# Graph layer with a maximum on one NeuronCore: gathered rows normalized on ScalarE instead of GpSimd, record ranks compared without a subtraction, a normalization's shifts in one operation

## What is computed

```python
h = max(layernorm(x), 0)
# layer 0: for every edge (row -> col)
feat = concat(h[col], h[row] - h[col])
messages = relu(feat @ W1 + b1) @ W2 + b2
x = x + segment_max(messages, col)          # 0 where a node has no edge
h = max(layernorm(x), 0)
# layer 1: averages of projected neighbours both ways, then a GRU cell
a_in  = segment_mean((h @ W_in.T + b_in)[src], dst)
a_out = segment_mean((h @ W_out.T + b_out)[dst], src)
x = x + gru_cell(concat(a_in, a_out), h)
```

## Time and profile before

| | us |
|---|---|
| median of three runs | 4011.75 |
| lowest and highest | 4011.28, 4018.98 |
| the profiled execution | 4021.37 |
| its span (first to last instruction) | 4019.6 |
| PE busy | 3058.4 (76%) |
| DVE busy | 3394.0 (84%) |
| ACT busy | 2061.9 (51%) |
| POOL busy | 2698.1 (67%) |

### The profile page before, as it was taken

The page is one execution under the profiler, slowest core; times in us unless marked ns, Lnnn a source line. Parts: engine busy times, 40 slices in busy tenths (PEclk is TensorE's granted clock), DMA queues, the critical chain, the costliest instruction groups (busy, mean ns, idle before and its releaser), DMA issues. The chain is left out here.

```text
span 4019.6 us, 91086 instructions
## 1 busy us (share of the span) xinstructions
PE 3058.4 (76%) x18561; PEld 1953.7 (49%) x18561; DVE 3394.0 (84%) x14919; ACT 2061.9 (51%) x4963; POOL 2698.1 (67%) x2895
## 2 busy tenths in 40 slices
PE   0244427777777777777777399999999999999998
PEld 0011116566555555555666255555555555555554
DVE  8844439999999999999999488888888888888888
ACT  0000017777677677767777144545544554555454
POOL 0266647777777777777777376666666666666664
...
GB/s 48 1 1 1 1 31 120 119 117 119 111 120 119 113 121 120 118 112 119 119 117 120 85 170 169 173 168 168 174 169 168 169 174 168 168 171 171 169 168 133
DMA packets 513673, 492.31 MB, mean 122 GB/s; under 512 B 218528, under 2 KB 487328, under 8 KB 513152
## 3 DMA queue, kind: packets, MB, share of 16 engines
...
## 5 line engine op out<-in xcount | busy, mean ns | idle before, releaser
L2536 POOL DMA_INDIRECT s_rows<-h_dram,s_idx x1044 | 989.3, 948 | 534.6 <-DVE s_idx L2743 277.3
L2111 POOL DMA_INDIRECT m_xg<-in_x_dram,m_idx x522 | 519.1, 994 | 143.8 <-issue 72.0
L2646 PE MATMUL sp_g<-s_wb,s_hT 128*128 128x512 f16 x2349 | 608.5, 379 | 0.0
L2659 PE MATMUL sp_g<-s_proj,s_onehot 128*128 128x384 f16 x3132 | 594.2, 326 | 0.0
L2636 PE MATMUL sp_p<-s_lhs,s_dT 128*128 128x384 f32 x1044 | 463.8, 526 | 93.6 <-DVE s_proj L2771 93.0
L2567 ACT ACTIVATE s_proj<-sp_p,s_share 128x384 f16<-128x384 f32 (+1 forms) x522 | 298.0, 571 | 377.6 <-PE sp_p L2636 377.6
L2120 POOL TENSOR_SCALAR m_h<-m_xg,m_mv,m_rs 128x128 f32<-128x128 f32 x522 | 477.9, 919 | 17.1 <-DVE m_rs L2319 6.4
L2127 POOL TENSOR_TENSOR m_q_rows<-m_x1s,m_h1s 128x384 f32<-128x384 f32 x261 | 259.7, 995 | 247.3 <-ACT m_h1s L2184 137.1
L710 POOL DMA_INDIRECT lists_src<-p_ent,p_pos x256 | 249.4, 974 | 254.8 <-issue 223.1
L2659 PEld LDWEIGHTS sp_g<-s_proj,s_onehot 128*128 128x128 f16 x3132 | 306.3, 98 | 231.2 <-issue 58.4
L2771 DVE SCALAR_TENSOR_TENSOR s_proj<-sp_p,s_share,s_proj 128x384 f16<-128x384 f32 (+1 forms) x522 | 320.1, 613 | 75.2 <-ACT s_proj L2567 75.2
...
...
## 6 DMA issues: line engine op xcount, KB each, us to landing
m_x<-in_x_dram SPq DMA_DIRECT2D x261, 192.0 KB
h_dram<-m_h1s SPq DMA_DIRECT2D x261, 192.0 KB
q_dram<-m_q_rows SPq DMA_DIRECT2D x261, 192.0 KB
s_h_rows<-h_dram SPq DMA_DIRECT2D x261, 192.0 KB
s_q_rows<-q_dram SPq DMA_DIRECT2D x261, 192.0 KB
out_dram<-s_out_rows SPq DMA_DIRECT2D x261, 192.0 KB
s_erow<-lists_dst SPq DMA_DIRECT2D x261, 128.0 KB
s_erow<-lists_src SPq DMA_DIRECT2D x261, 128.0 KB
```

The costliest lines, as they stand in the source:

```text
L2111: G_.indirect_dma_start(out=xg[:, st.slot(4), q, :], out_offset=None, in_=x[:, :], in_offset=bass.IndirectOffsetOnAxis(ap=idx[:, st.slot(4 ...
L2536: G_.indirect_dma_start(out=rows[:, s4, q, :], out_offset=None, in_=h1_dram[0:G * GROUP, :], in_offset=bass.IndirectOffsetOnAxis(ap=idx[:, ...
L2646: T.matmul(bank[:, t, :], hT[:, st.slot(4), of, t * P:(t + 1) * P], wb[:, w, :], start=(q == 0), stop=False, skip_group_check=True)
L2659: mm = T.matmul(ps_g[s2][:, t, 0:H3], onehot[:, st.slot(4), k, t * P:(t + 1) * P], proj[:, s2, k, w, :], start=False, stop=(k == 1 and w = ...
```

## The change

In `layer_max_sorted`, in four places:

- GpSimd's `normalize` is gone. ACT's `normalize` runs over five blocks instead of three; the last two come from `xg`. The semaphore `hg` is gone, and everybody who waited for it waits for five counts of `h` instead of three.
- `shifts` is one operation, minus one times `mv` times `rs`, over all five columns, in place of three operations on one column each. Both `mv` and `rs` are now inputs that are tensors; before, `rs` was a scalar read per partition.
- `shifts1` likewise, over three columns.
- `edge_ranks`, the tile `slot` and its semaphore are gone. `edge_slots` adds `first_rank` to `iota_slot` and compares with the record's own rank, with two scalars read per partition.

On DVE's list `(2, edge_ranks)` falls out and nothing else moves.

```diff
@@ gpsimd @@
                 def gather(st):
                     after(pool, "idx", st, per=2)
-                    after(pool, "h", st, per=3, back=4)
-                    after(pool, "hg", st, per=2, back=4)
+                    after(pool, "h", st, per=5, back=4)
...
-                def normalize(st):
-                    pool.wait_ge(S["rs"], st.count(4) - 3)
-                    after(pool, "tn", st, back=2)
-                    pool.sem_inc(S["go"], 1)
-                    for q in range(2):
-                        G_.tensor_scalar(h[:, st.slot(2), 3 + q, :], xg[:, st.slot(4), q, :], mv[:, st.slot(2), 3 + q, 0:1], rs[:, st.slot(4), 3 + q:4 + q],
-                                         ALU.subtract, ALU.mult).then_inc(S["hg"], 1)
...
-                fixed_loop(pool, G, [(6, gather), (8, normalize), (13, carried)], SPAN)
+                fixed_loop(pool, G, [(6, gather), (13, carried)], SPAN)
@@ scalar @@
                 def normalize(st):
-                    after(act, "rs", st, per=4)
+                    after(act, "rs", st, per=2)
                     after(act, "tn", st, back=2)
-                    for q in range(TILES):
-                        A.activation(h[:, st.slot(2), q, :], x3[:, st.slot(UN), q, :], ACT.Identity, bias=nm[:, st.slot(4), q:q + 1],
+                    for q in range(5):
+                        rows = x3[:, st.slot(UN), q, :] if q < TILES else xg[:, st.slot(4), q - TILES, :]
+                        A.activation(h[:, st.slot(2), q, :], rows, ACT.Identity, bias=nm[:, st.slot(4), q:q + 1],
                                      scale=rs[:, st.slot(4), q:q + 1]).then_inc(S["h"], 1)
@@ vector @@
-                def edge_ranks(st):
-                    landed(v, d_win, st)
-                    after(v, "sorted", st, back=UN)
-                    V.tensor_scalar(slot[:, st.slot(UN), :], win[:, st.slot(UN), :, 0], first_rank[:, bass.ds(st.t, 1)], None,
-                                    ALU.subtract).then_inc(S["slot"], 1)
-
                 def edge_slots(st):
                     after(v, "sorted", st, back=2)
-                    after(v, "slot", st)
+                    landed(v, d_win, st)
                     for c in range(SPREAD):
-                        V.tensor_scalar(oneh[:, st.slot(2), c, :], iota_slot[:, :], slot[:, st.slot(UN), c:c + 1], None,
-                                        ALU.is_equal).then_inc(S["oneh"], 1)
+                        V.tensor_scalar(oneh[:, st.slot(2), c, :], iota_slot[:, :], first_rank[:, bass.ds(st.t, 1)], win[:, st.slot(UN), c, 0:1],
+                                        ALU.add, ALU.is_equal).then_inc(S["oneh"], 1)
...
                 def averages(st):
                     after(v, "bn", st, per=5)
                     after(v, "std", st, back=2)
-                    after(v, "hg", st, per=2, back=2)
...
                 def scales(st):
                     after(v, "std", st)
-                    after(v, "h", st, per=3, back=4)
-                    after(v, "hg", st, per=2, back=4)
+                    after(v, "h", st, per=5, back=4)
...
                 def shifts(st):
-                    v.wait_ge(S["rs"], st.count(4) - 3)
-                    for q in range(TILES):
-                        V.tensor_scalar(nm[:, st.slot(4), q:q + 1], mv[:, st.slot(2), q, 0:1], rs[:, st.slot(4), q:q + 1], -1.0,
-                                        ALU.mult, ALU.mult).then_inc(S["rs"], 1)
+                    v.wait_ge(S["rs"], st.count(2) - 1)
+                    V.scalar_tensor_tensor(out=nm[:, st.slot(4), :], in0=mv[:, st.slot(2), :, 0], scalar=-1.0, in1=rs[:, st.slot(4), :],
+                                           op0=ALU.mult, op1=ALU.mult).then_inc(S["rs"], 1)
```

More of the change, by code:

```diff
@@ L1995, in layer_max_sorted @@
         iota_slot = sb("iota_slot", [P, P], F16)
-        slot = sb("slot", [P, UN, SPREAD])
         iota_loc = sb("iota_loc", [P, TILES, P], F16)
@@ L2175, in deviation1 @@
                     after(act, "mv1", st, per=3)
-                    after(act, "rs1", st, per=4, back=2)
+                    after(act, "rs1", st, per=2, back=2)
                     A.activation(std1[:, st.slot(2), :], mv1[:, st.slot(2), :, 1], ACT.Sqrt, bias=eps[:, :]).then_inc(S["std1"], 1)
                 def normalize1(st):
-                    after(act, "rs1", st, per=4)
+                    after(act, "rs1", st, per=2)
                     after(act, "q", st, back=4)
@@ L2210, in turn_rows @@
                 def turn_rows(st):
-                    after(pe, "h", st, per=3)
-                    after(pe, "hg", st, per=2)
+                    after(pe, "h", st, per=5)
                     after(pe, "hT", st, back=1)
@@ L2367, in shifts1 @@
                 def shifts1(st):
[L2368 to L2373 removed]
+                    v.wait_ge(S["rs1"], st.count(2) - 1)
+                    V.scalar_tensor_tensor(out=nm1[:, st.slot(2), :], in0=mv1[:, st.slot(2), :, 0], scalar=-1.0, in1=rs1[:, st.slot(2), :],
+                                           op0=ALU.mult, op1=ALU.mult).then_inc(S["rs1"], 1)
+                fixed_loop(v, G, [(12, add_x), (8, scales), (8, shifts), (12, statistics1), (5, row_numbers), (12, averages1),
                                   (10, one_hot), (2, edge_slots), (12, scales1), (12, shifts1), (10, run_maximum), (7, statistics), (10, gains),
```

11 lines of the change are left out of this document (3 added, 8 removed).

## The result

| | before | after |
|---|---|---|
| median, us | 4011.64 (4 runs, 4011.28 to 4018.98) | 3869.11 (4 runs, 3868.71 to 3870.66) |
| the profiled execution | 4021.4 | 3870.7 |
| its span | 4019.6 | 3868.9 |

The ratio is **0.9641**, with a 95% interval of 0.9625 to 0.9658: 142 us or 3.6% faster. The forecast was 3887, 18 us more than was measured, with the ring's own range at 3861 to 3923.

What follows compares the result with a forecast made beforehand. DVE was taken as the bound at 6.24 us per group; afterwards a 5.66 us ring plus 0.05 and 0.05 gives 5.76. Gain (6.24 - 5.76) x 260 = 125 us, so median 3887 us, range 3790 to 3965.

Steps and rivals of the forecast that it cites:

- the ring: Maximum layer: GpSimd's m_q_rows holds DVE's five-column m_nm, closing a loop DVE, ACT, GpSimd of 5.66 us per group; chance 0.60.
- long steps and late engines: Added to the 5.66 us turn: 0.05 for long steps, 0.05 for groups with a late engine, giving 5.76.
- the only case of a held operation: Next stage, trace before: DVE's two-column s_idx took 0.67 us beside a GpSimd tensor operation, where 149 ns is its median.
- m_rs behind m_x1s: On DVE, m_rs would start 0.45 us after m_x1s instead of 0.61, saving 0.16 per group; lower bound 0.
- m_onehot: On DVE, without GpSimd's m_h beside it, 0.48 us to the next start becomes about 0.33, saving 0.15.
- The second scalar: Four m_oneh on DVE read another scalar per partition: 0 to 0.05 us each, 0 to 0.20 together, 0.10 taken.
- The term for m_slot: Removing m_slot from DVE saves 0.14 us per group, at least; more where GpSimd held it up.
- No hold: Rival: GpSimd does not block the two-input m_nm; DVE and ACT set a 5.43 us step, 3801 us; chance 0.20.
- Lost mode: Rival: the added scalar also costs m_oneh its fast mode, 0.55 us per group; step 6.1, 3975 us; chance 0.11.
- Missed pause: Rival: held DVE misses GpSimd's 0.16 us pause and waits through the gather too; 4173 us; chance 0.05.
- Nothing: Rival: cover of DVE's other waits is thinner than thought, step stays near 6.2, 4010 us; chance 0.04.
- the first rival: The same as No hold: no blocking of m_nm by GpSimd, gain 211 us, 3801 us; chance 0.20.

Runs made afterwards that it cites:

- e7_add_zero: The kernel before, with m_oneh given a second operation that adds the constant 0 to iota; 4010.8 us, ratio 1.000.
- e6_ranks_only: The kernel before, with only the rank comparison changed: m_slot's subtraction gone, m_oneh reading two scalars per partition; 3998.9 us, ratio 0.997.
- e8_shifts_only: The kernel before, with only m_nm made in one operation each for five and three columns, GpSimd keeping its m_h; 3889.1 us, ratio 0.970.
- e9_move_only: The kernel after, with m_nm in single columns and m_slot's subtraction back, leaving only the gathered rows' normalization moved to ACT; 3974.9 us, ratio 0.992.
- e2_carried_memset: The kernel after, with GpSimd's sum into m_q_rows replaced by a fill with ones, same place and waits; 3834.4 us, ratio 0.957.
- e1_shift_late: The kernel after, with the five-column m_nm moved on DVE's list behind the second normalization's averages; 3807.9 us, ratio 0.949.
- e3_carried_twice: The kernel after, with GpSimd's sum made twice in a row, first into a tile nobody reads; 3880.7 us, ratio 0.968.
- e4_ranks_back: The kernel after, with m_slot's subtraction of ranks back and one scalar in m_oneh; 3878.7 us, ratio 0.967.

## Why the prediction was right

**The bound before.** 6.24 per group with DVE without gaps, ACT with room: right. e7_add_zero, which adds nothing to DVE's time, has the same step, and each part that took time off DVE in the kernel before shortened it (e6_ranks_only, e8_shifts_only, e9_move_only).

**The ring, term by term**, in the group shown above. It starts at the end of m_mv, 1121.46 + 0.31 = 1121.77.

| term | predicted | measured |
|---|---|---|
| to the end of m_h1s | 3.40 | 1123.93 + 1.25 - 1121.77 = 3.41 |
| to the start of m_q_rows and through it | 0.14 + 0.99 | 1125.26 - 1125.18 = 0.08, and 1.00 |
| DVE free before POOL's end | 0.05 | 1120.66 - 1120.61 = 0.05 |
| to the end of the next m_mv | 1.18 | 1121.77 - 1120.61 = 1.16 |
| turn | 5.66 | 5.60; step of this group 1125.10 - 1119.51 = 5.59 |

That DVE reaches m_nm inside m_q_rows was forecast for 3.9 to 4.1 into the turn; it was 4.00 (the next m_nm starts at 1125.77). The median step is 5.65. The mean is 5.67, 0.02 over it, where the prediction added **0.10** for long steps and late engines. That term was mis-sized, and it is the whole miss: (5.76 - 5.67) x 260 is 23 us, against 18 between 3887 and 3869 and 25 between the profiled executions. The steps of after are a little more even than those of before, whose mean is 0.04 over their median. That a small lateness of one engine falls in another's hold would explain it; no run tests that.

**m_nm.** Right: 0.08 apart for the three columns (mean 0.10) and 0.08 for the five where nothing holds them (e2_carried_memset), against 0.10 taken and 0.07 to 0.17 as bounds. Moved away from m_rs the five take 0.05 (e1_shift_late). Held, 0.43. The prediction calls the only case of a held operation; the trace of before has 163 s_idx that start inside POOL's s_diff, of which ten are held, for up to 745 ns, and end 0.03 after it (median). So its ground was firmer than it knew.

**m_rs behind m_x1s.** Forecast 0.45, measured 1119.96 - 1119.51 = 0.45. The register operation behind the wait was worth its 0.15: in before the 204 turns with it stand at 0.605, and 29 turns outside of the loop, which lack it, at 0.451.

**m_onehot.** Forecast 0.33, measured 1121.99 - 1121.69 = 0.30; its longest is 503 ns instead of 828. Right in kind: in before it took 627 ns in the median where it started inside POOL's m_h (149 groups), which is gone.

**The second scalar.** This is the step that failed in size: bounds 0 to 0.05 each, 0.025 taken, **0.06** measured. The lower bound came from a guess that the second would be read along with the first, the upper from the difference of two lines of other types with two columns, which need not be the price of a scalar alone. It makes 0.24 per group where 0.10 was taken. The term for m_slot erred the other way: 0.14 was taken and called the least, and its mean was 0.215, with another 0.06 at the m_mv ahead of it. So DVE without the hold needs 5.59 - (1120.61 - 1120.18 - 0.08) = 5.24 in this group, within the 5.17 to 5.37 named, in part because the two errors offset each other. In the ring neither shows in the time: DVE stands 0.35 us per group in the hold, more than both errors together.

**ACT and the waits.** Two more m_h cost 1123.93 - 1123.16 = 0.77, as forecast. ACT waits 54.8 + 12.1 = 66.9 us for m_mv in the window's 236 groups, 0.28 per group; 0.3 was forecast.

**DMA** was to rise from 0.62 to 0.67 and fell to 0.59, at 131 GB/s instead of 117. The forecast scaled the share with the rate; the share also counts how long packets take, and that shrank for the gathers (from 1000 to 1900 their queue took 20.6% of the engines' time for 20.64 MB, before it 26.1% for 18.56 MB). It was no bound, so nothing hung on it.

**POOL's work.** 1.00 + 0.96 + 0.94 is 2.9 per group, and 3.4 with the two pauses of 0.15 and 0.31 between them; 3.2 was said.

**The rivals.** No hold: refuted by m_nm's 516 ns with its end always at that of m_q_rows, and by e1_shift_late and e2_carried_memset, which take the hold away. Lost mode: refuted by 0.223 apart and by e6 and e7. Missed pause: refuted by e3_carried_twice. Nothing: refuted by the time. What the first rival would have given, 3801, is close to what e1_shift_late took when it opened the ring, 3808, but not by the same sum: that kernel also saves the 0.15 us of its new place and pays for new waits.

## What to carry to other kernels

Before an operation on DVE gets a second tensor of SBUF as input, look at where it starts against GpSimd's own operations on tensors, in the kernel as it will be after the change: the saving of some instructions can be given back as a hold, and the hold closes a ring through engines that each have idle time. An edit is then best tested together with its place: here moving one entry of a list was worth 61 us (35 of it can be had by taking the hold away alone) and changing a second 48 more, and the second was worth nothing before the first. In a ring, what one engine saves isn't seen in the time but in how long it is held, so its "busy" share must be read with the durations of single operations.

## What the runs showed of the chip

- A second scalar that DVE reads per partition has a price that adds up: 61 ns (295 against 234 ns), with 128 columns of two bytes going no slower otherwise. A constant as second operand of the same instruction costs nothing (234 against 233).
- A two-input operation of DVE held by GpSimd gets its turn even between two GpSimd operations with no pause between them (e3_carried_twice: 1122.40 + 1.00, next 1123.36, DVE on at 1123.35).
- Beside GpSimd's sum of two tensors the hold is whole, not shared: m_nm of 0.16 becomes what is left of m_q_rows from its start on, plus 0.02, 0.50 in the group shown and up to 0.71 in after. Beside GpSimd's tensor_scalar m_h it is not whole. In e8_shifts_only the three-column m_nm starts inside an m_h in 241 groups, mostly 0.25 in, and takes 211 ns in the median instead of 163; it is through 0.33 ahead of the end of m_h, which takes 0.82 (median of one). The prediction's reading, that the later one waits for the whole of the other, doesn't hold there; what lets it go was not tried. The line over the stage:

```profile
L2368 DVE SCALAR_TENSOR_TENSOR m_nm<-m_mv,m_rs x261: 160/211/464, 597.9 to 2088.0; 128x3 f32<-128x3 f32 x131
```

- Beside a gather the five-column m_nm is not held: in e1_shift_late it starts inside one in 244 groups and takes 128 to 177 ns, in e8_shifts_only in 244 groups and 162 to 182 ns. In before, s_idx starts inside a gather nine times; eight take 149 to 160 ns, and the ninth is the case of the earlier trace rows with 777. What made it different stays open.
- m_oneh (one tensor input, two bytes) is held by a gather, but only by its later part. In after the 475 that start in the first 0.38 us of a gather take 303 ns in the median and 316 at the most. Another 250 start later with at least 0.33 of the gather left; 244 of them are held, to 0.02 after its end (median), and take 370 ns in the median and up to 568.
- Gathers issued a turn earlier took a smaller share of the DMA engines in both pairs (0.68 against 0.77 on e1_shift_late, 0.51 against 0.59 on after) at no fewer bytes per second. The place of the gathers isn't all there is to it: with them where after has them, the share in the same stretch is 0.52 in e3_carried_twice and 0.70 in e4_ranks_back, at 130 and 132 GB/s. What the packets had waited for was not tried.
